# Repeated mask products on TensorE at the barriers, and the first square in another order

## The chip, the cores and the metric

The kernel runs on one core of a Trainium2 chip. The metric is the device time of one execution in microseconds (us), taken as the median of several runs. All products are exact enough for fp32 inputs, so most matrices are split into a high and a low part of type fp32r, and a product is three matrix products: high by high, low by high and high by low.

## The reference

`x` is (16, 512, 128): 16 batches, N = 512 nodes, D = 128. `adj` is (512, 512), sparse and symmetric in pattern. Four graph layers follow each other, each as `x = layernorm(x + layer(x))`. In short:

```
# layer 0: eight Euler steps of a diffusion
h = x @ fc_in_w.T + fc_in_b
for _ in range(8):
    f = 0.5 * sigmoid(alpha)[:, None] * (adj @ h - h) + h @ w_eff - h + x
    h = h + f / 8                      # w_eff = w * clip(d, 0, 1) @ w.T
# layer 1: two graph convolutions with ReLU, then LSTMs over windows of 1 to 4 nodes
# layer 2: normalized adjacency, 128 -> 256, batch norm, ReLU, 256 -> 128, batch norm
h = relu(batchnorm((A_hat @ x) @ W1.T + b1)); out = batchnorm(h @ W2.T + b2)
# layer 3: attention over 256 edges (src, dst), four heads
Y = segment_sum(softmax_by_src(leaky_relu(Xq[src] + Xq[dst]) . a + log(adj[src, dst])) * Xv[dst], src)
out = Y @ W_out.T
```

The changed kernel computes the same.

## The kernel before

`x` stays in SBUF from start to end. The program is four blocks, one after another, and all engines meet at a barrier between two blocks.

1. **`phase_operators`** (to about 63 us). It builds what layer 0 needs as operators. With L = kappa * adj + diagonal, it makes the transposed powers `LT0`, `LT1` (the square) and `LT2` (the third power), each split in high and low parts (`LT0h`, `LT0l`), and powers of the 128x128 operator R in `RP`. ACT makes the high parts, DVE the low parts of the powers (`split`), POOL the low part `Ll` of L itself. DVE also computes the row sums of adj (`row_sums`), from which the vectors `pair` and `U` are made. `l_power(r, j)` is one tile of a power: 4 chunks k, three products each, written out in the helper `product` (L65 to L67). The order of the tiles is a list (`order`), a bank of PSUM is a tile's place in it modulo 8, and PE's program below is written out by hand in that order: transpose of w (L465), transposes of L by chunk (L469), R (L474), `l_power(2, 0)`, and so on.
2. **`phase_main`** (about 63 to 832 us). Layers 0 and 1 and the first half of layer 2, in an order that a planner in the program sets. It also makes the edge masks `GZ` and `GsT` (names `z_GZ`, `z_GsT` in the profile), matrices of zeros and ones with few ones, of type fp32r. The change doesn't touch this block.
3. **`phase_batchnorm`** (about 832 to 871 us). DVE and POOL make the batch norm's scale and shift, ACT writes the normalized hidden layer `U` (L1875), PE multiplies it by `W2T` (L1861; both are f32, and such a product runs as two passes, each an instruction in the trace), DVE adds the bias (L1914) and takes statistics (L1907), and at the end makes scale and shift of the second batch norm (L1895 to L1901, with POOL). PE uses banks 4 to 7 here.
4. **`phase_attention`** (from 871 us). Layer 3, in an order from `first_part`, `slot` and `drain`; each engine walks the one list and takes its own items. For the part around the change: `z` is ACT's normalization of a batch (L2256), `T` PE's transposes of it (L2168), which DVE adds to X (L2328), then statistics (`s3`), variances (`v3`), POOL's root (`p3`, L2434), DVE's shift (`sh3`, L2350), the application on ACT and DVE (`ap3`, L2284 and L2380), the split of x (`xs`: ACT's high part, POOL's low part `aXL`), and `G`, PE's gather by the masks (L2177, eight products). T3 or G0 below is the item with its batch number.

Of the kernel before, what the change touches and what calls it, by code (L numbers as in the profile page):

```python
# [16 lines left out]
P = 128  # L17
# [45 lines left out]
def product(pe, out, lhs, rhs, start=True, stop=True):  # L63

    pe.matmul(out, lhs[0], rhs[0], start=start, stop=False)  # L65
    pe.matmul(out, lhs[0], rhs[1], start=False, stop=False)  # L66
    return pe.matmul(out, lhs[1], rhs[0], start=False, stop=stop)  # L67


def low_part(eng, out, full, high):  # L70
# [14 lines left out]
def phase_operators(nc, sh, d):  # L85
# [12 lines left out]
    C, D, N = sh.C, sh.D, sh.N  # L98
    with ExitStack() as ctx:
# [154 lines left out]
        def _(dve):  # L254
# [53 lines left out]
            for c in range(C):  # L308
# [6 lines left out]
            link(dve.tensor_scalar(dclip[:, :], dcol[:, :], 0.0, 1.0, ALU.max, ALU.min))  # L315
            dve.tensor_scalar(wTd[:, :], wT[:, :], dclip[:, 0:1], DT, ALU.mult, ALU.mult)\
                .then_inc(S["dve_tile"], 1)
            row_sums(0, 2)
            for j in range(C):
                split(f"LT{j}")  # L320
            copy("R", RP[:, 1, :], bank("R")[:, 0:D])
            link(row_sums(2, C))
            link(dve.tensor_tensor(pair[:, :, 1], sh.rs[:, :], kappa[:, :], ALU.mult))
            dve.wait_ge(S["memsets"], 5)
            link(dve.tensor_tensor(pair[:, :, 1], pair[:, :, 1], ldiag[:, :], ALU.add))
# [87 lines left out]
        def _(pe):  # L413
# [9 lines left out]
            def r_power(name, k, n, needs):  # L423
                begin(name, [needs])
                done(pe.matmul(bank(name)[:, 0:n * D], RP[:, k, :], RP[:, 1:n + 1, :], start=True, stop=True))

            def l_power(r, j):
                begin(f"L{r}T{j}", [] if r == 2 else [f"L{r - 1}T{C - 1}"])
                for k in range(C):
                    rows = slice(j * P, (j + 1) * P)  # L430
                    if r == 2 and j == 0:
                        pe.wait_ge(S["ll_done"], k + 1)
                        pe.wait_ge(S["dve_tile"], at[f"LT{k}"] + 1)
                    ins = product(pe, bank(f"L{r}T{j}"), (Lh[:, k, rows], Ll[:, k, rows]),
                                  (sh.LT[r - 2][0][:, k, :], sh.LT[r - 2][1][:, k, :]),
                                  start=(k == 0), stop=(k == C - 1))
                done(ins)
# [25 lines left out]
            pe.wait_ge(S["w_in"], 16)  # L463
            pe.wait_ge(S["idn"], 1)
            done(pe.transpose(bank("wT")[:, 0:D], w_nat[:, :], sh.ident[:, :]))  # L465
            for c in range(C):
                pe.wait_ge(S["l_done"], c + 1)
                for j in range(C):
                    ins = pe.transpose(bank(f"LT{j}")[:, c * P:(c + 1) * P], L[:, c, j * P:(j + 1) * P],  # L469
                                       sh.ident[:, :])  # L470
                    if c == C - 1:
                        done(ins)
# [1335 lines left out]
def phase_batchnorm(nc, sh, d):  # L1808
# [8 lines left out]
    with ExitStack() as ctx:  # L1817
# [35 lines left out]
        @block.tensor  # L1853
        def _(pe):
            def second(i, last):
                for b in range(QB):
                    n = QB * i + b
                    wait(pe, S["o_out"], n - QB + 1)
                    for j in range(J):
                        pe.wait_ge(S["u_done"], J * n + j + 1)  # L1860
                        ins = pe.matmul(sh.psum[:, 4 + b, :], sh.W2T[:, j, :], U[:, J * b + j, :], start=(j == 0),  # L1861
                                        stop=(j == J - 1))
                    ins.then_inc(S["o_mm"], 1)

            peeled(pe, NQ, second)

        @block.scalar
        def _(act):
# [86 lines left out]
def phase_attention(nc, sh, d, out):  # L1955
# [8 lines left out]
    with ExitStack() as ctx:  # L1964
# [34 lines left out]
        def first_part():  # L1999

            return [("z", 0), ("z", 1), ("T", 0), ("z", 2), ("s3", 0), ("v3", 0), ("p3", 0), ("T", 1), ("z", 3), ("s3", 1),
                    ("v3", 1), ("p3", 1), ("T", 2), ("z", 4), ("sh3", 0), ("ap3", 0), ("xs", 0), ("s3", 2), ("v3", 2),
                    ("sh3", 1), ("ap3", 1), ("xs", 1), ("p3", 2), ("T", 3), ("s3", 3)]

        def slot(k):
# [147 lines left out]
        @block.tensor  # L2153
        def _(pe):
            def begin_dve(item):
                n = dve_ring[item]
                wait(pe, S["dve_free"], n - len(DVE_BANKS) + 1)

            def begin_act(item):
                n = act_ring[item]  # L2160
                wait(pe, S["act_free"], n - len(ACT_BANKS) + 1)

            def turned(n):
                pe.wait_ge(S["z_done"], n + 1)
                begin_dve(("T", n))
                for c in range(C):
                    cols = slice(c * P, (c + 1) * P)
                    ins = pe.transpose(dve_bank(("T", n))[:, cols], tmp[:, n % QB, cols], sh.ident[:, :])  # L2168
                ins.then_inc(S["pe_dve"], 1)

            def gather(n):
                pe.wait_ge(S["xl_done"], n + 1)
                begin_act(("G", n))
                for c in range(C):
                    cols = slice(c * D, (c + 1) * D)
                    for part in (XH, XL):
                        ins = pe.matmul(act_bank(("G", n)), part[:, n % 2, cols], GZ[:, c, :, :],  # L2177
                                        start=(c == 0 and part is XH), stop=(c == C - 1 and part is XL))
                ins.then_inc(S["pe_act"], 1)

            def project_edges(n):
                pe.wait_ge(S["act_free"], act_ring["G", n] + 1)
                begin_act(("U", n))
                to = act_bank(("U", n))
                pe.matmul(to[:, 0:NE], WT[:, 0, :], Z[:, n % QB, 0:NE], start=True, stop=True)
                for k in range(K):
                    cols = slice(NE + k * P, NE + (k + 1) * P)
                    ins = pe.matmul(to[:, cols], Z[:, n % QB, cols], WT[:, 1, :], start=True, stop=True)
                ins.then_inc(S["pe_act"], 1)

            def scores(n):
                b = n % QB
                if b == 0:
                    wait(pe, S["sc_done"], n // QB)
                pe.wait_ge(S["lr_done"], n + 1)
                pe.matmul(sh.psum[0:R, 7, 0:NE], wide[:, R - NH - NH * b:2 * R - NH - NH * b], lr[:, b, :],
                          start=(b == 0), stop=(b == QB - 1)).then_inc(S["sc_mm"], 1)

            def attention_turned(g):
                to = dve_bank(("at", g))  # L2200
                pe.wait_ge(S["ex_done"], g + 1)
                begin_dve(("at", g))
                for k in range(K):
                    ins = pe.transpose(to[:, k * R:(k + 1) * R], s2[:, g, k * P:(k + 1) * P], sh.ident[0:R, 0:R])
                ins.then_inc(S["pe_dve"], 1)

            def denominators(g):
                to = dve_bank(("dn", g))
                pe.wait_ge(S["dve_free"], dve_ring["at", g] + 1)
                begin_dve(("dn", g))  # L2210
                for k in range(K):
                    for j in range(K):
                        ins = pe.matmul(to[:, k * R:(k + 1) * R], same[:, j, k * P:(k + 1) * P],
                                        exT[:, g, j * R:(j + 1) * R], start=(j == 0), stop=(j == K - 1))
                ins.then_inc(S["pe_dve"], 1)

            def scatter(n):
                pe.wait_ge(S["va_lo"], n + 1)
                begin_act(("S", n))
                for k in range(K):  # L2220
                    for part in (vah, val):
                        ins = pe.matmul(act_bank(("S", n)), part[:, n % QB, k, :], GsT[:, k, :],  # L2222
                                        start=(k == 0 and part is vah), stop=(k == K - 1 and part is val))
                ins.then_inc(S["pe_act"], 1)

            def project(n):
                pe.wait_ge(S["act_free"], act_ring["S", n] + 1)
                begin_dve(("P", n))
                for c in range(C):
                    cols = slice(c * P, (c + 1) * P)  # L2230
                    ins = pe.matmul(dve_bank(("P", n))[:, cols], Y[:, n % QB, cols], WT[:, 2, :], start=True, stop=True)  # L2231
                ins.then_inc(S["pe_dve"], 1)

            for kind, n in order:
                if kind == "T":
                    turned(n)
                elif kind == "G":
                    gather(n)
                elif kind == "U":
                    project_edges(n)  # L2240
                elif kind == "W":
                    scores(n)
                elif kind == "at":
                    attention_turned(n)
                elif kind == "dn":
                    denominators(n)
                elif kind == "S":
                    scatter(n)
                elif kind == "P":
                    project(n)  # L2250
# [278 lines left out]
```

## Time and profile before

| what | value |
|---|---|
| median of 3 runs | 1007.44 us (1007.18 to 1009.31) |
| the profiled execution | 1006.96 us |
| its span, first to last instruction | 1005.2 us |
| mean granted TensorE clock | 0.981 |
| PE busy | 922.8 us, 92% |
| PE weight loads | 792.2 us, 79% |
| DVE busy | 658.7 us, 66% |
| ACT busy | 546.1 us, 54% |
| POOL busy | 311.8 us, 31% |
| DMA | 31.62 MB, mean 31 GB/s |

The profile is one execution. A time in a row is counted from the start of the span. A row of the timeline is a group of like instructions: start, duration of the group, engine, line of the program, operation, output and input by name, shape, count, and in brackets how long the engine was idle before it and what it waited for. Durations of PE instructions include the way through the array, so the distance from one start to the next is what a product costs in a row of products. The granted clock is a share of full speed: 1.00 is 2.4 GHz, 0.50 is 1.2 GHz.

### The profile page before, as it was taken

How to read it: one execution, taken by the hardware profiler on the slowest of the kernel's cores; microseconds unless marked ns; L12 is line 12 of the kernel's file. 1: busy time of each engine (PE TensorE's matmuls, PEld its weight loads, DVE VectorE, ACT ScalarE, POOL GpSimd, SP SyncE). 2: the span in 40 equal slices, each digit the busy share in tenths (PEclk: the TensorE clock that was granted, in tenths of full speed). 3: DMA queues.
4: the chain of work that ended last, by engine and by line, in shares of the span. 5: the costliest groups of instructions: out<-in, count | busy, mean ns of one | idle time of the engine just before them, and what ended most of it. 6: DMA issues, size and time to landing. Idle time of an engine off the chain costs nothing. (4 is left out here: it accounts for less than half of the span.)

```text
span 1005.2 us, 14453 instructions
## 1 busy us (share of the span) xinstructions
PE 922.8 (92%) x5144; PEld 792.2 (79%) x5144; DVE 658.7 (66%) x1627; ACT 546.1 (54%) x1136; POOL 311.8 (31%) x290
## 2 busy tenths in 40 slices
PE   6999997999998999999999999899989987678994
PEld 4689986899997888998889899788778863356773
DVE  6664435445546646665655775698897876778877
ACT  2043224655645565554656464557667647466757
POOL 3011222331233233223323323224333220145663
PEclk9989999999999999999999999999999998889998
DMA  8030011001010100101010010301000000000014
GB/s 225 1 82 2 22 53 74 1 22 42 1 43 2 42 22 1 42 2 43 1 43 22 1 43 1 124 1 62 15 31 22 1 1 0 1 0 1 2 43 126
DMA packets 33994, 31.62 MB, mean 31 GB/s; under 512 B 8450, under 2 KB 28034, under 8 KB 33924
## 3 DMA queue, kind: packets, MB, share of 16 engines
q1 hardware_dynamic: 32900, 30.64, 9.9%
q8 instruction: 41, 0.67, 0.3%
q14 instruction: 29, 0.24, 0.1%
q10 hardware_dynamic: 960, 0.07, 0.1%
q0 software_dynamic: 64, 0.00, 0.0%
HBM read 22.83 MB, written 7.87 MB: 31 GB/s over the span
## 5 line engine op out<-in xcount | busy, mean ns | idle before, releaser
L1322 ACT ACTIVATE gates<-psum,gbias 128x256 f32<-128x256 f32 (+2 forms) x312 | 158.9, 565 | 63.5 <-PE psum L67 58.7
L65 PE MATMUL psum<-LS,WI 128*128 128x256 f32 (+2 forms) x312 | 104.1, 334 | 10.0 <-ACT gates L1322 6.3
L67 PE MATMUL psum<-LS,WI 128*128 128x256 f32 (+2 forms) x312 | 102.9, 330 | 0.0
L66 PE MATMUL psum<-LS,WI 128*128 128x256 f32 (+2 forms) x312 | 102.8, 330 | 0.0
L72 POOL TENSOR_TENSOR LS<-A,LS 128x512 fp32r<-128x512 f32 (+2 forms) x44 | 48.9, 1112 | 172.2 <-ACT LS L1307 172.1
L72 POOL TENSOR_TENSOR LS<-Hodd,LS 128x512 fp32r<-128x512 f32 (+2 forms) x44 | 48.8, 1109 | 147.5 <-ACT LS L1307 147.5
L72 DVE TENSOR_TENSOR yl<-psum,yh 128x512 fp32r<-128x512 f32 x58 | 39.6, 689 | 65.0 <-ACT yh L1264 44.2
L72 POOL TENSOR_TENSOR XSl<-X,XSh 128x512 fp32r<-128x512 f32 x32 | 42.3, 1324 | 115.8 <-ACT XSh L1259 115.8
L1329 ACT ACTIVATE tc<-cell 128x512 f32<-128x512 f32 (+2 forms) x88 | 45.3, 514 | 57.8 <-DVE cell L1617 33.7
L65 PEld LDWEIGHTS psum<-LS,WI 128*128 128x128 f32 x312 | 59.2, 190 | 19.5 <-POOL LS L72 10.2
L65 PE MATMUL psum<-B2h,LT2h 128*128 128x256 f32 x256 | 72.7, 284 | 1.0 <-DVE X L1435 1.0
L67 PE MATMUL psum<-B2h,LT2l 128*128 128x256 f32 x256 | 72.4, 283 | 0.0
L66 PE MATMUL psum<-B2l,LT2h 128*128 128x256 f32 x256 | 72.4, 283 | 0.0
L66 PEld LDWEIGHTS psum<-LS,WI 128*128 128x128 f32 x312 | 59.2, 190 | 5.0
L67 PEld LDWEIGHTS psum<-LS,WI 128*128 128x128 f32 x312 | 59.3, 190 | 4.2
L65 PE MATMUL psum<-LS,WH 128*128 128x256 f32 (+2 forms) x192 | 60.1, 313 | 0.0
L66 PE MATMUL psum<-LS,WH 128*128 128x256 f32 (+2 forms) x192 | 59.9, 312 | 0.0
L67 PE MATMUL psum<-LS,WH 128*128 128x256 f32 (+2 forms) x192 | 59.9, 312 | 0.0
L65 PE MATMUL psum<-Eh,yh 128*128 128x384 f32 x168 | 56.6, 337 | 0.0
L67 PE MATMUL psum<-Eh,yl 128*128 128x384 f32 x168 | 56.3, 335 | 0.0
L66 PE MATMUL psum<-El,yh 128*128 128x384 f32 x168 | 56.2, 335 | 0.0
L548 DVE BATCH_NORM_STATS2 nstats<-X 128x6 f32<-128x128 f32 x256 | 54.2, 278 | 0.4
(368 smaller groups left out, 2674.3 us busy)
## 6 DMA issues: line engine op xcount, KB each, us to landing
WI<-lstm_weights SPq DMA_DIRECT2D x14, 512.0 KB, 3.5
WH<-lstm_weights SPq DMA_DIRECT2D x11, 512.0 KB, 4.5
X<-in_x SPq DMA_DIRECT2D x16, 256.0 KB, 5.4
out<-X SPq DMA_DIRECT2D x16, 256.0 KB, 2.3
lstm_weights<-WI SPq DMA_DIRECT2D x4, 512.0 KB, 2.6
lstm_weights<-WH SPq DMA_DIRECT2D x3, 512.0 KB, 2.7
A<-in_adj SPq DMA_DIRECT2D x4, 256.0 KB, 4.5
z_A<-in_adj SPq DMA_DIRECT2D x1, 1024.0 KB, 5.2
```

What stands on the lines that cost most here:

```text
L65: pe.matmul(out, lhs[0], rhs[0], start=start, stop=False)
L66: pe.matmul(out, lhs[0], rhs[1], start=False, stop=False)
L67: return pe.matmul(out, lhs[1], rhs[0], start=False, stop=stop)
L72: return eng.tensor_tensor(out, full, high.bitcast(F32), ALU.subtract)
L548: return dve.bn_stats(self.stats[:, bass.ds(self.sh.C * n + c, 1), :], self.sh.X[:, c, bass.ds(n, 1), :])
L1322: act.activation(gates[:, gate, 0:n], sh.psum[:, gate, 0:n], ACT.Tanh if gate == G else ACT.Sigmoid, bias=gbias[:, p_ - 1, gate:gate + 1]) ...
L1329: act.activation(tcs[:, 0:n], cell[:, s % 2, 0:n], ACT.Tanh).then_inc(S["tanh_done"], 1)
```

## The change

A helper `keep_busy` issues n products into a bank that nothing reads at that time. It is called

- in `phase_operators`, five times after the transpose of w and twice before the transposes of chunk 2, identity by identity (f32, 128 columns), into the bank of `R2`, which a later product overwrites;
- in `phase_batchnorm`, 12 times before the first projection product and 16 times after the last, `GsT` by `GZ` (fp32r, 512 columns), into bank 0;
- in `phase_attention`, 24 times behind T2, as a new item `busy` of the list, into bank 7.

The first tile of the square (`first_square`) takes its four high-by-high products first and then the products with a low part. DVE's first two row sums move from before the low parts to behind them.

```
+def keep_busy(pe, out, lhs, rhs, n):
+    for _ in range(n):
+        pe.matmul(out, lhs, rhs, start=True, stop=True)
...
-            row_sums(0, 2)
             for j in range(C):
                 split(f"LT{j}")
             copy("R", RP[:, 1, :], bank("R")[:, 0:D])
-            link(row_sums(2, C))
+            link(row_sums(0, C))
...
+            def first_square(rows):
+                to, (high, low) = bank("L2T0"), sh.LT[0]
+                for k in range(C):
+                    pe.wait_ge(S["lh_done"], k + 1)
+                    pe.wait_ge(S["hi_done"], his.index(f"LT{k}") + 1)
+                    pe.matmul(to, Lh[:, k, rows], high[:, k, :], start=(k == 0), stop=False)
+                for k in range(C):
+                    pe.wait_ge(S["ll_done"], k + 1)
+                    pe.matmul(to, Ll[:, k, rows], high[:, k, :], start=False, stop=False)
+                    pe.wait_ge(S["dve_tile"], at[f"LT{k}"] + 1)
+                    ins = pe.matmul(to, Lh[:, k, rows], low[:, k, :], start=False, stop=(k == C - 1))
+                done(ins)
...
             def l_power(r, j):
                 begin(f"L{r}T{j}", [] if r == 2 else [f"L{r - 1}T{C - 1}"])
+                rows = slice(j * P, (j + 1) * P)
+                if r == 2 and j == 0:
+                    first_square(rows)
+                    return
                 for k in range(C):
-                    rows = slice(j * P, (j + 1) * P)
-                    if r == 2 and j == 0:
-                        pe.wait_ge(S["ll_done"], k + 1)
-                        pe.wait_ge(S["dve_tile"], at[f"LT{k}"] + 1)
...
             done(pe.transpose(bank("wT")[:, 0:D], w_nat[:, :], sh.ident[:, :]))
+            idle = bank("R2")[:, 0:P]
+            keep_busy(pe, idle, sh.ident[:, :], sh.ident[:, :], 5)
             for c in range(C):
+                if c == 2:
+                    keep_busy(pe, idle, sh.ident[:, :], sh.ident[:, :], 2)
                 pe.wait_ge(S["l_done"], c + 1)
...
+            masks = sh.GZ[:, 0, :, :]
+            keep_busy(pe, sh.psum[:, 0, :], sh.GsT[:, 0, 0:P], masks, 12)
             peeled(pe, NQ, second)
+            keep_busy(pe, sh.psum[:, 0, :], sh.GsT[:, 0, 0:P], masks, 16)
...
-                    ("v3", 1), ("p3", 1), ("T", 2), ("z", 4), ("sh3", 0), ...
+                    ("v3", 1), ("p3", 1), ("T", 2), ("busy", 0), ("z", 4), ("sh3", 0), ...
...
+                elif kind == "busy":
+                    keep_busy(pe, sh.psum[:, 7, :], GsT[:, 0, 0:P], GZ[:, 0, :, :], 24)
```

PE's own order at the start of `phase_operators`, before; `x16` are the transposes of L, and the three lines repeat for the four chunks:

```order
L465 MATMUL psum<-ident,w_nat 128x128
L469 MATMUL psum<-ident,L 128x128 x16
L474 MATMUL psum<-wT,wTd 128x128
L65 MATMUL psum<-LT0h,Lh 128x512
L66 MATMUL psum<-LT0l,Lh 128x512
L67 MATMUL psum<-LT0h,Ll 128x512
```

and now, with what each waits for (`hi_done` is ACT's high parts of the powers, `lh_done` and `ll_done` are the parts of L, `dve_tile` counts DVE's tiles):

```order
L73 MATMUL psum<-ident 128x128 x5
L491 MATMUL psum<-ident,L 128x128 [waits l_done]
L491 MATMUL psum<-ident,L 128x128 x3
...
L73 MATMUL psum<-ident 128x128 x2
L491 MATMUL psum<-ident,L 128x128 [waits l_done]
...
L496 MATMUL psum<-wT,wTd 128x128 [waits dve_tile]
L437 MATMUL psum<-LT0h,Lh 128x512 [waits hi_done,lh_done] x4
L440 MATMUL psum<-LT0h,Ll 128x512 [waits ll_done]
L442 MATMUL psum<-LT0l,Lh 128x512 [waits dve_tile]
```

Seven repeats are new, the four high products no longer wait for DVE, and the low ones alternate behind them.

PE's order at the end of the projection and the start of attention, now:

```order
L1883 MATMUL psum<-U,z_W2T 128x512 x8
L73 MATMUL psum<-z_GZ,z_GsT 128x512 x16
L1839 UNCONDITIONAL_BRANCH
L2178 UNCONDITIONAL_BRANCH
L2193 MATMUL psum<-ident,A 128x128 x12
L73 MATMUL psum<-z_GZ,z_GsT 128x512 x24
L2193 MATMUL psum<-ident,A 128x128 x4
L2202 MATMUL psum<-z_GZ,aXH 128x512
```

Before, the last eight projection products were followed by the two branches, 16 transposes in a row (T0 to T3) and G0. Now 16 repeats stand ahead of the branches and 24 between T2 and T3.

## Rows read from the trace of the kernel before

**Rows 1.** Busy time by stretch of TensorE: stretch, length, PE busy (count), granted clock, DMA.

```profile
13.45:18.98 5.53, 5.53 (x14) 1.00 1.20 290
...
834.77:841.59 6.82, 5.48 (x7) 0.50 0.00 0
...
868.90:875.73 6.83, 3.67 (x16) 0.50 0.00 1
875.73:879.14 3.41, 0.00 (x0) 1.00 0.00 0
879.14:885.97 6.83, 4.51 (x13) 0.50 0.00 0
```

**Rows 2.** Timeline of PE in the first 20 us.

```profile
7.90 1.97 PE L469 MATMUL psum<-ident,L 128*128 128x128 f32 x8 [1.04 <-DVE L L312]
10.36 1.12 PE L469 MATMUL psum<-ident,L 128*128 128x128 f32 x4 [0.49 <-DVE L L312]
11.57 0.79 PE L474 MATMUL psum<-wT,wTd 128*128 128x128 f32 x2
13.45 0.77 PE L65 MATMUL psum<-LT0h,Lh 128*128 128x512 f32 x1 [1.08 <-DVE LT0l L72]
14.01 0.63 PE L66 MATMUL psum<-LT0l,Lh 128*128 128x512 f32 x1
...
18.28 0.63 PE L67 MATMUL psum<-LT0h,Ll 128*128 128x512 f32 x1
...
19.54 0.40 PE L67 MATMUL psum<-LT0h,Ll 128*128 128x512 f32 x1
19.77 0.39 PE L65 MATMUL psum<-LT0h,Lh 128*128 128x512 f32 x1
```

**Rows 3.** Timeline of the other engines, 10.5 to 14.5 us.

```profile
10.40 1.11 DVE L316 TENSOR_SCALAR wTd<-wT,dclip 128x128 f32<-128x128 f32 x1
10.88 2.06 ACT L244 ACTIVATE LT0h<-psum 128x512 fp32r<-128x512 f32 x4
11.44 1.27 DVE L298 TENSOR_REDUCE rs<-A 128x1 f32<-128x512 f32 x2
...
12.63 2.47 DVE L72 TENSOR_TENSOR LT0l<-psum,LT0h 128x512 fp32r<-128x512 f32 x4
```

**Rows 4.** Waits of PE between 13 and 62 us; the answer's other row is the 1.08 above.

```profile
PE psum L446 <- DVE U L72: 0.9, 1, 0.9
```

**Rows 5.** Timeline from the barrier at 832 us into the projection.

```profile
832.54 1.04 DVE L1895 BATCH_NORM_AGGREGATE bmv<-z_st 128x2 f32<-128x96 f32 x2 [0.32 <-PEq L621]
...
835.24 7.15 ACT L1875 ACTIVATE U<-z_hidden,bsh,bsc 128x512 f32<-128x512 f32 x10 [3.75 <-DVE bsh L1901]
...
836.11 14.13 PE L1861 MATMUL psum<-U,z_W2T 128*128 128x512 f32 x26 [5.34 <-ACT U L1875]
...
854.80 11.75 PE L1861 MATMUL psum<-U,z_W2T 128*128 128x512 f32 x27
```

**Rows 6.** Timeline from the projection's end over the barrier at 871 us.

```profile
861.67 4.88 PE L1861 MATMUL psum<-U,z_W2T 128*128 128x512 f32 x11
...
870.48 0.16 DVE L1901 TENSOR_TENSOR bsh<-z_par,bsh 128x1 f32<-128x1 f32 x1
...
872.02 3.67 PE L2168 MATMUL psum<-ident,A 128*128 128x128 f32 x16 [5.47 <-ACT A L2256]
```

**Rows 7.** Timeline of the start of attention.

```profile
881.46 0.80 PE L2177 MATMUL psum<-z_GZ,aXH 128*128 128x512 f32 x1 [5.77 <-POOL aXL L72]
...
882.25 0.68 DVE L2328 TENSOR_TENSOR X<-psum,X 128x512 f32<-128x512 f32 x1
...
884.66 1.00 POOL L2434 TENSOR_TENSOR n3scale<-n3work,const 128x4 f32<-128x4 f32 x1
...
885.04 1.50 PE L2168 MATMUL psum<-ident,A 128*128 128x128 f32 x8
...
886.13 1.29 DVE L2328 TENSOR_TENSOR X<-psum,X 128x512 f32<-128x512 f32 x2 [2.29 <-PE psum L2168]
...
887.34 0.15 DVE L2350 SCALAR_TENSOR_TENSOR n3shift<-n3work,n3scale 128x4 f32<-128x4 f32 x1
```

More of the change, by code:

```diff
@@ L2001, in first_part @@
             return [("z", 0), ("z", 1), ("T", 0), ("z", 2), ("s3", 0), ("v3", 0), ("p3", 0), ("T", 1), ("z", 3), ("s3", 1),
-                    ("v3", 1), ("p3", 1), ("T", 2), ("z", 4), ("sh3", 0), ("ap3", 0), ("xs", 0), ("s3", 2), ("v3", 2),
+                    ("v3", 1), ("p3", 1), ("T", 2), ("busy", 0), ("z", 4), ("sh3", 0), ("ap3", 0), ("xs", 0), ("s3", 2), ("v3", 2),
                     ("sh3", 1), ("ap3", 1), ("xs", 1), ("p3", 2), ("T", 3), ("s3", 3)]
```

## The prediction

> **What bounds the kernel now.** I read the granted clock by stretch first [rows 1], then the timeline of TensorE (PE) at the places where the clock is low. After its start the kernel is a chain in which PE is busy 92% of the span, so time that PE loses in front of its own work is mostly time of the span. The clock column says 0.50 from 834.77 to 841.59, from 868.90 to 875.73 and from 879.14 to 885.97 [rows 1]. Each of these begins after a pause of PE and ends after a run of steady work: 836.11 to 841.59 (5.5 us), 872.02 to 875.73 (3.7), 881.46 to 885.97 (4.5) [rows 5, 6, 7].
>
> At the very start the column misleads. It says 1.00 for 13.45 to 18.98, but ten products from 14.01 to 18.28 are 0.427 us apart, and the same shape is 0.23 us apart at 19.54 to 19.77 [rows 1, 2]. 512 columns in 0.427 us are the 1.2 GHz level, in 0.23 us the 2.4 GHz level; so this stretch is at half clock too, and the clock rose near 18.98, after 5.5 us of steady work. The Trainium skill, "TensorE: Matmul & The Clock Gate", Part 1, says that half clock is the default state, released by activity, and warns that recorded clock events can be unreliable; the spacing agrees. By the column instead, the first term below would be only the wait removed, 1.4 us.
>
> **Term 1, the start.** Before, PE ends the transposes of L at 11.48, computes R from 11.57 in two passes, and then waits 1.08 us for the first low part, since DVE does two row sums (1.27 us) ahead of it [rows 2, 3]. The first square starts at 13.45. Now its four high products come first, and need only ACT's high parts: the first is there at 11.48 (10.88 plus 0.6), the fourth at 12.94. R holds PE to 12.0, so the square starts at 12.0, 1.45 us earlier. The low parts start on DVE when wTd is done at 11.51, and the fourth is there near 14.0 (2.47 us for four [rows 3]); at 0.427 us per product PE asks for it near 16.7, at full clock near 14.5. All four row sums (2.5 us) now stand between R's copy and U. DVE is at R's copy at 14.0, so U is there near 17.7; PE wants it behind the second square, near 18 or later. That is close but covered; if PE runs at full clock from 12.2 it may wait some tenths.
>
> The repeats themselves: five 128-column f32 products after the transpose of w take about 0.43 us each (R, the same form, has its two passes 0.2 us apart [rows 2]), 2.1 us from about 2.9 to 5.1, before L is there at 5.7: no cost. Two more take 0.85 us between 8.75 and 9.6. They push the last transposes from 10.36 to about 10.45, and R waits for wTd at 11.51 anyway: at most 0.1 us.
>
> If the clock still rises at 18.98, 1.45 us of added half-clock work is worth 0.7 us. Each us by which it rises earlier adds 0.5 us. With the repeats PE is steadily busy from 7.90 to 11.3, and after a pause of 0.2 us from 11.57 on. The runs before a rise were 3.7 to 5.5 us, 4.8 in the mean: counted from 11.57 the rise is at 16.4 (gain 2.0), counted from 7.90 at 12.7 (gain 3.6, where the low parts begin to bind). I take a rise near 15.2: 0.7 + 0.5 x 3.8 = **2.6 us**. Bounds 0.7 and 3.6. Behind this, PE has one more wait up to 62 us, 0.89 us for U [rows 4], which hangs on PE's own products, and so moves with them. Nothing later waits for a time of day: the shift passes the barrier near 63.
>
> **Term 2, the second projection.** PE ends at 830.77 (836.11 less 5.34), engines leave the barrier at about 832.5, ACT gives its first U after 835.24, one per 0.72 us [rows 5]. Twelve mask products (form 128x512 fp32r, 0.23 us at full clock [rows 2]) fill 832.6 to 835.4. Two pauses of 1.8 and 0.7 us stay where one of 5.3 was. At full clock a pass takes 0.43 us (11.75 us for 27 [rows 5]), two per product, 0.87 against ACT's 0.72 per U, so PE is the limit from its first product on, and the cold 5.48 us [rows 1, 5] hold 2.74 us of full-clock work. **2.7 us** gained; bounds 2.7, and 0.9 if the clock falls in the 1.8 us pause: repeats then take 0.427 us each, end at 837.7 (1.6 late plus some 0.2), with the clock rising about then.
>
> **Term 3, the start of attention.** Sixteen mask products behind the last projection take 3.7 us, from 866.2 to 869.9; DVE's statistics end at 870.64 [rows 6]. So PE reaches the barrier 0.6 us before DVE: no cost. At half clock they would take 6.8 us and hold the barrier up by 2.4. A pause of 2.1 us stays to 872.02 in place of 5.47 [rows 6]. Transposes at full clock are ready about 0.4 us earlier (four at 0.21 us, halved), and DVE starts at 872.8 in place of 873.2. Then 24 mask products, 5.6 us at full clock from 873.9, end at 879.5. T3 stands behind them; DVE wants it at 882.25 [rows 7], so 2.7 us of slack cover them. G0 waits for POOL's low part at 881.46 less 0.4, and its eight products take 1.9 us in place of 3.6 [rows 7]. T4 and T5 stand behind G0, and DVE waits 2.29 us for T4 [rows 7]: this wait nearly goes. Late next is POOL's root, 885.66 less 0.4; the shift that DVE made at 887.34 comes at about 885.3 to 885.5. **1.9 us**. If the clock falls in the 2.1 us pause, the repeats themselves warm it: they end near 881.5, G0 starts 0.5 late but is quick, gain 1.2. Bounds 0 and 2.0.
>
> **Sum.** 2.6 + 2.7 + 1.9 = 7.2 us. The profiled execution took 1006.96 us, so 999.8; the median of the three runs lies 0.5 above it, and against that I say **1000.2 us**. The removed waits are no engine's work elsewhere, but low-clock stretches that the change doesn't touch can fall elsewhere when everything shifts; one us either way.
>
> **Rivals.**
> *Pauses too long.* The clock falls in both remaining pauses. For: it fell 2.4 us after PE's last product at 866.55 (861.67 plus 4.88) [rows 1, 6]. Against: at 830.77 it took 4.0 us. Terms 0.9 and 1.2, with 2.6 at the start: 1002.7.
>
> *Start only shifts.* The clock at the start rises no sooner, since neither the identity products nor the steadier run bring the rise forward; 0.7 to 1.4 us in place of 2.6: 1001.7.
>
> *Quiet repeats (slower).* Products of mask by mask, nearly all zeros, do not hold the clock up, and it is low through them. Then the twelve take 5.1 us and end 1.6 us late; at the end of the projection about 0.3 us hangs over DVE; and the 24, from 874.8, take 10.2 us to 885.1. T3 and G0 then start near 885.5, 4.5 us late where before T3 was in time. 1.6 + 0.3 + 4.5 less 1.4 at the start is +5.0: 1012.4. It decides if the 24 are spaced 0.427 us to their end: above about 0.35 us apart they outlast the slack of T3. Against: G0 has the same masks as moving operand and the clock rose within it [rows 1, 7]; but there the other operand was dense.
>
> *No net change.* Time shifted forward is lost again in a longer cold stretch behind the barrier near 63 or in the pause of attention, or U comes late. The Trainium skill, same page and part, reports that one kernel had 6, 11 or 14 cold products from run to run, and puts the whole ramp below 1% of a span; here 12 of the first square were cold, within that. By 6 alone the cold loss at the start would be 1.2 us. Time 1006.5. No row shows such a second execution.
>
> **Chances.** Forecast 0.60 (its own range 998.0 to 1002.0), pauses too long 0.16, start only shifts 0.10, no net change 0.08, slower 0.06. A measurement of this kernel tells 0.2%, 2.0 us, from no change: faster 0.86, same 0.08, slower 0.06. The range 997.2 to 1004.3 takes in the forecast with its bounds and the two rivals of partial gain, and leaves out the last two.
>
> **What would show it.** In the changed profile: the square's first product near 12.0 and 0.23 us spacing from about 15; granted clock 1.00 from 830 to 870, first projection product 0.75 us behind the twelve, U products 0.43 us per pass at once; 24 repeats 0.23 us apart, ended before 880; G0 in 1.9 us; DVE's wait for T4 under 0.5 us. Wrong would be: repeats spaced 0.427 us throughout (slower), PE behind DVE at a barrier, DVE or PE waiting for U near 18.

## The result, and the profile after

Eight executions of each kernel: median 1000.98 us (998.36 to 1004.92) with the change, 1007.31 us without it. The medians are 6.3 us apart. The ratio of all executions is 0.9926, 95% interval 0.9899 to 0.9954: faster by 4.6 to 10.2 us, under 1%. The forecast was 1000.2 us. The profiled execution took 1001.52 us. Of the later executions of the kernel before, two lie far outside the rest (1170.59 and 3196.63 us) and are in no comparison.

The head of its page, against 922.8 us of PE and a span of 1005.2 us before:

```profile
span 999.7 us, 14585 instructions
PE 934.2 (93%) x5210; PEld 803.4 (80%) x5210; DVE 658.8 (66%) x1627; ACT 545.4 (55%) x1136; POOL 312.3 (31%) x290
```

PE is busy 11.4 us longer in a span that is 5.5 us shorter: the repeats are added work. The stretches of the granted clock in the changed kernel (columns as in [rows 1]):

```profile
12.38:15.57 3.19, 3.19 (x7) 0.50 1.19 299
15.67:18.98 3.31, 3.31 (x17) 1.00 1.20 290
60.19:63.45 3.26, 3.26 (x16) 0.50 0.23 58
476.44:479.85 3.41, 3.41 (x11) 0.50 0.00 0
732.53:735.94 3.41, 3.18 (x11) 0.51 0.00 0
810.91:814.32 3.41, 3.41 (x9) 0.51 0.00 0
829.50:868.90 39.40, 35.24 (x97) 1.00 0.01 1
868.98:872.38 3.40, 3.40 (x12) 0.50 0.00 0
...
971.38:974.78 3.40, 3.40 (x18) 0.50 0.27 77
```

The whole projection with both pauses around it, 829.50 to 868.90, now runs at the 2.4 GHz level. At the start of attention the clock still falls, at 868.98, but comes back 3.4 us later, where before it was low from 868.90 to 875.73 and again from 879.14 to 885.97 [rows 1]. Three cold stretches (stretches at 0.50) are new against the profile before: near 476, near 811 and near 971.

The timeline of PE at the start, the counterpart of [rows 2]:

```profile
2.95 2.34 PE L73 MATMUL psum<-ident 128*128 128x128 f32 x10
6.01 1.97 PE L491 MATMUL psum<-ident,L 128*128 128x128 f32 x8 [0.72 <-DVE L L318]
7.77 1.06 PE L73 MATMUL psum<-ident 128*128 128x128 f32 x4
8.62 0.70 PE L491 MATMUL psum<-ident,L 128*128 128x128 f32 x4
11.14 0.66 PE L491 MATMUL psum<-ident,L 128*128 128x128 f32 x4 [1.82 <-DVE L L318]
...
12.38 2.22 PE L437 MATMUL psum<-LT0h,Lh 128*128 128x512 f32 x4 [0.36 <-ACT LT0h L250]
...
16.84 0.38 PE L430 MATMUL psum<-RP 128*128 128x128 f32 x2
```

The seven repeats are fourteen passes, in 2.34 and 1.06 us with the way through the array; 2.1 and 0.85 were costed. In this execution they did bring the clock up: four transposes take 0.70 us at 8.62, against 1.12 us for four at 10.36 [rows 2], and the two passes of R take 0.39 us, against 0.79. But PE waits 1.82 us for the last chunk of L, the clock falls at 12.23, and the first seven products of the square are cold again. The steady run the forecast counted on, from 7.90 on, did not come about.

PE from the second barrier on:

```profile
831.46 3.00 PE L73 MATMUL psum<-z_GZ,z_GsT 128*128 128x512 f32 x12 [1.77 <-PEq L643]
835.03 27.73 PE L1883 MATMUL psum<-U,z_W2T 128*128 128x512 f32 x64 [0.57 <-ACT U L1900]
862.20 4.23 PE L73 MATMUL psum<-z_GZ,z_GsT 128*128 128x512 f32 x16
868.23 2.67 PE L2193 MATMUL psum<-ident,A 128*128 128x128 f32 x12 [1.80 <-ACT A L2283]
870.55 6.60 PE L73 MATMUL psum<-z_GZ,z_GsT 128*128 128x512 f32 x24
876.99 0.60 PE L2193 MATMUL psum<-ident,A 128*128 128x128 f32 x4
877.35 0.48 PE L2202 MATMUL psum<-z_GZ,aXH 128*128 128x512 f32 x1
```

The pause of 5.34 us [rows 5] is now 1.77 and 0.57 us. The 64 passes of the projection take 27.73 us, 0.43 us apart from the first. The sixteen repeats end at 866.43, and DVE's last instruction of the block ends at 866.85, the first row below, so they hold up nothing. The 24 repeats, the first few of them slow, end at 877.15, just before G0's input is there: POOL's low part ends at 877.21. DVE at these places:

```profile
866.69 0.16 DVE L1926 TENSOR_TENSOR bsh<-z_par,bsh 128x1 f32<-128x1 f32 x1
...
879.91 1.37 DVE L2355 TENSOR_TENSOR X<-psum,X 128x512 f32<-128x512 f32 x2 [0.27 <-PE psum L2193]
881.51 0.16 DVE L2377 SCALAR_TENSOR_TENSOR n3shift<-n3work,n3scale 128x4 f32<-128x4 f32 x1 [0.22 <-POOL n3scale L2461]
```

DVE's wait for T4 fell from 2.29 us [rows 7] to 0.27, and the shift for batch 2 now waits for POOL's root, as forecast.

### The profile page after: what moved, and what is told of

It reads as the page before. It is cut to its first block and busy times, and to the rows that moved or that the text cites. A ratio compares the mean times of both kernels' runs of the same rounds, so it can differ in the third digit from the quotient of the medians.

```text
span 999.7 us, 14585 instructions
## 1 busy us (share of the span) xinstructions
PE 934.2 (93%) x5210; PEld 803.4 (80%) x5210; DVE 658.8 (66%) x1627; ACT 545.4 (55%) x1136; POOL 312.3 (31%) x290
```

## Six stages, read from every profile

One profile can't separate terms of 2 us from the scatter of single executions, which is as large. The kernel before alone had times near 1005.4, 1007.4, 1010.4 and 1012.6 us in 34 executions beside the first experiments. So each profile is cut at the same instructions. Each column is the difference of two start times in it:

- start: 0 to the R product behind the square's first tile
- second: from there to PE's first product of the main block
- main: to the last widening product of that block
- projection: its first product to T0
- head: T0 to DVE's shift for batch 2
- tail: from there to the end of the span

Between the main block's last product and the projection's first lie 5.74 us that no column holds (7.37 in `e7_rows4`).

```
kernel            start  second   main   projection   head    tail
before            18.71   44.52  767.14     35.91     15.32  117.86
e12_before_again  18.74   44.45  774.87     35.83     15.27  117.90
e1_start          15.94   43.37  771.62     34.84     14.80  117.89
e5_square         16.48   43.35  767.17     35.90     15.32  117.84
e6_ident          18.47   44.63  768.97     34.73     14.74  117.82
e2_projection     17.70   43.36  769.10     33.21     15.38  117.91
e3_attention      17.88   43.37  769.11     34.84     13.27  120.49
after             16.84   43.35  769.09     33.20     13.28  118.19
e4_full           16.46   43.35  769.35     33.21     13.30  119.60
e11_full_again    16.05   43.37  768.88     33.20     13.25  119.50
e9_plus           15.36   43.55  769.87     33.20     13.24  117.83
e10_plus          15.35   44.03  771.45     33.20     13.25  118.57
e7_rows4          15.83   43.38  771.54     36.69     18.89  119.60
e8_double         16.20   43.36  769.22     33.21     18.30  120.77
```

The main block, which the change doesn't touch, took 767.1 to 774.9 us. What differs there is how often the clock fell: once in `before` (736) and `e5_square` (732), three times in `after` (476, 732, 811), five times in `e1_start` and `e7_rows4`. From one fall to three is 2.0 us, to five 4.4 us, so a fall there costs 1.0 to 1.1 us.

## The experiments

### The parts alone

`e1_start` keeps the identity repeats, the square's new order and the moved row sums, and has no mask products:

```
-            keep_busy(pe, sh.psum[:, 0, :], sh.GsT[:, 0, 0:P], masks, 12)
-            keep_busy(pe, sh.psum[:, 0, :], sh.GsT[:, 0, 0:P], masks, 16)
-                    ("v3", 1), ("p3", 1), ("T", 2), ("busy", 0), ("z", 4), ...
+                    ("v3", 1), ("p3", 1), ("T", 2), ("z", 4), ...
```

> The start part alone: seven identity repeats, the first square with its high products first, DVE's row sums behind. Theory (terms add): 1.5 to 3 us faster than before; in the profile the second tile of the square starts near 17.0 instead of 18.98, and this lead is kept to the first barrier. Rival (the start is absorbed later): the lead is seen at 20 us and gone at 63 us, and the time is within 0.5 us of before. The cold stretches at 836 and 879 stay as before.

Measured: ratio 0.9979 (0.9962 to 0.9996), 2.1 us faster. Start stage 15.94 us against 18.71, and the lead stays: second stage 43.37. The rival of an absorbed start falls. The cold stretches at the barriers did not stay as before, though nothing there was changed: the one in the projection was 3.4 us long and not 6.8, and that stage took 34.84 us.

`e2_projection` has only the first of these three edits left in, and the start as before.

> Only the twelve mask products ahead of the projection. Theory: granted clock stays 1.00 from 832 to 868, the 64 projection passes take 27.7 us instead of 30.4, 2.7 us faster than before. Rival (another cold stretch takes its place): passes as quick, but the time less than 1 us faster.

Measured: ratio 0.9986 (0.9965 to 1.0007). Its two rows of PE:

```profile
832.33 3.01 PE L73 MATMUL psum<-z_GZ,z_GsT 128*128 128x512 f32 x12 [1.77 <-PEq L647]
...
835.90 27.73 PE L1887 MATMUL psum<-U,z_W2T 128*128 128x512 f32 x64 [0.57 <-ACT U L1903]
```

The mechanism is exactly as stated: 27.73 us of passes. The stage is 33.21 us; in the six profiles without the twelve repeats it is 34.7 to 35.9, 35.3 in the mean. So the term is 2.1 us in the mean, and 2.7 where the cold stretch is as long as in the first profile. The time, 1.4 us faster, agrees with that, but its interval reaches no change, so the time alone does not decide against the rival.

`e3_attention` has only the sixteen and the 24 repeats.

> Only the sixteen mask products behind the projection and the 24 behind T2. Theory: G0 starts at once at full clock, DVE's shift for batch 2 comes 16 us behind the barrier's exit less 2, DVE waits under 0.5 us for T4; 1.5 to 2 us faster than before. Rival (the repeats hold T3 and G0 up): G0 starts later than before relative to the barrier and nothing is gained.

Measured: ratio 1.0000 (0.9979 to 1.0022): nothing. Yet the head stage is 13.27 us against 14.7 to 15.4 in the six kernels without these repeats, the forecast 1.9 us. What went wrong stands in the tail, 120.49 us against 117.9. Three cold stretches of it:

```profile
894.04:897.44 3.40, 3.40 (x9) 0.50 0.00 0
917.92:924.76 6.84, 6.84 (x24) 0.50 0.00 0
975.96:979.36 3.40, 3.40 (x18) 0.50 0.27 77
```

The clock falls there in the thin part of attention, where PE waits for DVE and POOL again and again for 0.5 to 1.3 us. Not every fall costs time. The falls of all profiles, in us behind the shift for batch 2, with the start of the last of the sixteen gathers and the end of the span counted from the same shift (a fall 110 to 113 us behind it, near the end of the span, is in every profile and left out):

```
profiles                               falls (length)                last gather    tail
before, e12_before_again, e5_square    none                          72.0 to 72.1   117.84 to 117.90
e1_start, e6_ident                     90 (3.4)                      72.0 to 72.1   117.82, 117.89
after                                  90 (3.4)                      72.0           118.19
e2_projection, e9_plus                 9 (3.4)                       72.1           117.91, 117.83
e10_plus                               10 (3.4)                      72.8           118.57
e4_full, e11_full_again, e7_rows4      35 (3.4), 90 (6.8)            72.7           119.50 to 119.60
e3_attention, e8_double                10 (3.4), 34 (6.8), 92 (3.4)  74.2 to 74.3   120.49, 120.77
```

The fall near 894, the first of the three rows, costs nothing: two profiles have one there and the old tail. The fall 34 to 35 us behind the shift delays the later gathers by 0.7 us where it is 3.4 us long, and by 2.2 where it is 6.8; with a 6.8 us stretch near 90 another 1.0 to 1.1 is lost.

In the six profiles without these repeats the tail was 117.82 to 117.91 us; in the five with the 24 full-height repeats as the change has them (`e3_attention`, `after`, `e4_full`, `e11_full_again`, `e9_plus`) it was 117.83 to 120.49, 119.1 in the mean. So 1.2 of the 1.9 us are given back on average, more than all of it in `e3_attention` and nothing in `e9_plus`. Without the repeats DVE's shift for batch 2 came 1.0 to 2.0 us behind a rise of the clock in all six, since G0, whose end releases it, was itself slow until that rise. With them it stands in no fixed relation to a rise. That this is why the costly falls never came before is an argument from these profiles, not shown by an edit.

`e4_full` is the changed kernel.

> The changed kernel again, as the sum to hold the three parts against on one chip. Theory (terms add): 6 to 8 us faster than before, the sum of the three parts within 2 us. In its profile the clock falls in other pauses of the main block than in the run before the prediction, by up to two more or fewer stretches of 1.6 to 1.7 us each.

Measured: ratio 0.9944 (0.9925 to 0.9963), 5.6 us faster; the three parts alone gave 2.1, 1.4 and 0.0. The whole is just under the 6 to 8 us expected. The sum, 3.5 us, is 2.1 below the whole, just outside the margin of 2 given and inside what their intervals leave. There were cold stretches near 476, 732 and 811 as in `after`.

### What does the work at the start

`e5_square` is `e1_start` without the seven identity repeats.

```
-            keep_busy(pe, idle, sh.ident[:, :], sh.ident[:, :], 5)
-                if c == 2:
-                    keep_busy(pe, idle, sh.ident[:, :], sh.ident[:, :], 2)
```

> The start part without its identity repeats: only the order of the square and the moved row sums. Theory (the repeats bring the clock up earlier): the square starts near 12.2, 1.2 us earlier than before, but the clock rises only after four to six us of it, and the second product of R (the one behind the square's first tile) starts at 16.8 to 17.6, later than the 15.9 to 16.8 with repeats. Rival (the order alone does it): as early as with repeats, 16.4 or sooner.

`e6_ident` is the reverse, also without mask products: the identity repeats, with the square and the row sums of before.

```
+            row_sums(0, 2)
             for j in range(C):
                 split(f"LT{j}")
...
-            link(row_sums(0, C))
+            link(row_sums(2, C))
...
-                    first_square(rows)
+                    for k in range(C):
+                        pe.wait_ge(S["ll_done"], k + 1)
+                        pe.wait_ge(S["dve_tile"], at[f"LT{k}"] + 1)
+                        ins = product(...)
```

> The identity repeats with the square and the row sums in the old order. Theory: the square starts at 13.2 to 13.5 as before, and the second product of R starts near 17.0 to 17.8, against 17.7 to 18.7 in the kernels with the old start. Rival (the repeats do nothing): 17.7 or later and a cold square of at least ten products.

PE in `e5_square`, then in `e6_ident`:

```profile
11.51 0.80 PE L493 MATMUL psum<-wT,wTd 128*128 128x128 f32 x2
11.96 2.05 PE L437 MATMUL psum<-LT0h,Lh 128*128 128x512 f32 x4
```

```profile
9.38 1.44 PE L498 MATMUL psum<-ident,L 128*128 128x128 f32 x8 [0.94 <-DVE L L318]
11.48 0.80 PE L503 MATMUL psum<-wT,wTd 128*128 128x128 f32 x2 [0.66 <-DVE wTd L322]
13.36 0.77 PE L65 MATMUL psum<-LT0h,Lh 128*128 128x512 f32 x1 [1.08 <-DVE LT0l L78]
```

Without repeats the square starts at 11.96, where the forecast put it (12.0), and the start stage is 16.48 us, sooner than the 16.8 to 17.6 expected and close to the 16.4 of the rival, that the order alone does it. With the repeats alone it is 18.47, with eleven cold products in the first square: that is what the rival named, that the repeats do nothing. In that execution the clock was up early, eight transposes in 1.44 us against 1.97 in [rows 2], and was low again by R, whose two passes take 0.80 us. The four kernels with the old start have 18.71, 17.70, 17.88 and 18.74, mean 18.3; the eight with the whole new start 15.35 to 16.84, mean 16.0. By the one profile of `e5_square`, the order of the square and the moved row sums carry about 1.8 of 2.3 us. What the identity repeats add, at most 0.5 us, is within the scatter of single profiles and stays open.

### Rows, not time: the price of repeats that do not count

`e7_rows4` narrows all mask repeats to 4 partition rows, and changes nothing else.

```
-            masks = sh.GZ[:, 0, :, :]
+            masks = sh.GZ[0:4, 0, :, :]
...
-            keep_busy(pe, sh.psum[:, 0, :], sh.GsT[:, 0, 0:P], masks, 12)
+            keep_busy(pe, sh.psum[:, 0, :], sh.GsT[0:4, 0, 0:P], masks, 12)
...
-                    keep_busy(pe, sh.psum[:, 7, :], GsT[:, 0, 0:P], GZ[:, 0, :, :], 24)
+                    keep_busy(pe, sh.psum[:, 7, :], GsT[0:4, 0, 0:P], GZ[0:4, 0, :, :], 24)
```

> All three groups of mask repeats with 4 partition rows instead of 128, the same count and columns. Theory of the change as first stated (TensorE only has to be busy): as the changed kernel, clock 1.00 through the projection, 33.2 us from the first projection product to T0. Rival (products of few rows do not hold the clock, as in the stretch of 4-row products from 57.3 us on, at whose end it fell while PE was busy): the clock falls during the twelve, these take up to 5.1 us and the projection starts up to 1.6 us late and is cold for some us; the 24 take up to 10.2 us and G0 comes 12 to 14 us behind T0 instead of 9.1; total about 1006 to 1011 us. This is also the price of the rival of quiet repeats in the prediction.

PE in its timeline, the 4-row products written as 4*128, and the granted clock of two stretches:

```profile
832.92 5.27 PE L73 MATMUL psum<-z_GZ,z_GsT 4*128 4x512 f32 x12 [1.77 <-PEq L643]
838.12 7.15 PE L1883 MATMUL psum<-U,z_W2T 128*128 128x512 f32 x10
...
868.38 5.29 PE L73 MATMUL psum<-z_GZ,z_GsT 4*128 4x512 f32 x16
...
877.56 10.60 PE L73 MATMUL psum<-z_GZ,z_GsT 4*128 4x512 f32 x24
888.10 1.12 PE L2193 MATMUL psum<-ident,A 128*128 128x128 f32 x4
```

```profile
832.00:842.30 10.30, 9.38 (x17) 0.55 0.01 2
870.70:891.20 20.50, 19.36 (x54) 0.50 0.00 1
```

One execution, 1015.14 us, above the 1006 to 1011 expected; its main block, which the edit doesn't touch, was one of the long ones, and one execution of the kernel before beside it took 1014.22 us, so only the stages tell here. The clock was low for 20.5 us in a row although PE was busy 19.4 of them. It fell at 870.67 within the sixteen, with PE busy: most of the first ten start 0.23 us apart, the last six 0.427. The twelve took 5.27 us and the 24 took 10.60, T0 to the shift became 18.9 us, and the projection 36.7 us plus 1.6 us before it. These are the forecast's prices of its slower rival: 5.1 us, 10.2 us, and T3 and G0 some 4.5 us late. Only the question whether the change's own repeats count was answered the other way. The Trainium skill, "TensorE: Matmul & The Clock Gate", section "LDWEIGHTS (loading the stationary operand)", says that the row count does not matter for the time of a weight load. The trace agrees: at the low clock a load of 4 rows took 0.326 us, and a full-height one of the same mask 0.331 (the first slow ones of the 24 in `after`). The products, too, are 0.427 us apart at that clock at either height. But for the clock the height mattered in this pair of runs.

`e8_double` doubles the 24.

```
-                    keep_busy(pe, sh.psum[:, 7, :], GsT[:, 0, 0:P], GZ[:, 0, :, :], 24)
+                    keep_busy(pe, sh.psum[:, 7, :], GsT[:, 0, 0:P], GZ[:, 0, :, :], 48)
```

> 48 instead of 24 repeats behind T2; the rest as changed. Theory (the 24 are covered since DVE wants T3 only later): the 48 end 5.6 us later, T3 is 4 to 5 us late for DVE, G0 starts 14.2 to 14.8 us behind T0 instead of 9.1 and DVE's shift for batch 2 about 17.5 to 18.5 instead of 13.3: 4 to 5 us slower than the changed kernel. Rival (PE time is free there): no more than 1 us later.

PE, then DVE:

```profile
870.04 12.01 PE L73 MATMUL psum<-z_GZ,z_GsT 128*128 128x512 f32 x48
881.89 0.60 PE L2193 MATMUL psum<-ident,A 128*128 128x128 f32 x4
```

```profile
882.53 0.69 DVE L2355 TENSOR_TENSOR X<-psum,X 128x512 f32<-128x512 f32 x1 [4.90 <-PE psum L2193]
```

G0 came 14.5 us behind T0 and the shift 18.3 us, 5.0 us later than with 24. So 24 repeats are free and 48 are not. How much slack is left behind the 24 depends on the clock: in `after`, where the first ones are slow, next to none, and in `e3_attention`, with the clock up, PE still waited 1.05 us for POOL ahead of G0.

### A version with more of it

`e9_plus` adds repeats in two pauses of the main block:

```
+                if b == 11 and j == 0:
+                    begin(n)
+                    keep_busy(pe, bank(n), sh.WT[0][:, 0, :], bn["AhTh"][:, 0, :], 11)
...
+                if q == NQ - 1 and k == first_step(3) + 1:
+                    wait(pe, gate_act[G], NS * q + uses(k, G))
+                    keep_busy(pe, sh.psum[:, G, :], sh.WT[0][:, 0, :], bn["AhTh"][:, 0, :], 10)
                 pe.wait_ge(S["xs_done"], NS * q + k + 1)
```

> The changed kernel with repeats in two more pauses, both in the main block: ten ahead of the second LSTM step of window 3 in the last quarter (the pause of 2.6 us near 733), eleven ahead of the widening of batch 11 (the pause of 2.7 us near 810). Full-height operands, into a bank that the next product overwrites. Theory (a pause of TensorE over about 2 us costs a cold stretch of 3.4 us, 1.6 to 1.7 us of time, in most executions): the clock no longer falls near 732 and 810, the main block takes 1.6 to 3.3 us less, and the time is 1.5 to 3.3 us below the changed kernel's. Rival (the fall is only moved on): another cold stretch within 20 us, less than 1 us gained.

Two rows of PE, and one stretch of the clock:

```profile
732.99 4.13 PE L73 MATMUL psum<-z_AhTh,z_WTh 128*128 128x512 f32 x10 [2.49 <-ACT gates L1350]
736.96 0.32 PE L65 MATMUL psum<-LS,WI 128*128 128x340 f32 x1
```

```profile
806.00:815.00 9.00, 8.81 (x38) 1.00 0.00 0
```

Ratio to before 0.9936 (0.9915 to 0.9956), median 1000.2 us, beside `e11_full_again` with 1000.4 and 0.9944: no difference that can be told. The main block took 769.87 us against 768.88 in `e11_full_again`, where 1.6 to 3.3 us less were expected: in this execution the clock also fell near 153 and 638. And by the main blocks above a fall there costs 1.0 to 1.1 us, not 1.6 to 1.7. The pause of about 2 us in the theory is no measured limit either: a pause of 1.80 us ahead of T0 was followed by a fall in `after`, and one of 2.74 us near 812 by none in the first profile of before. Near 810 it did what was expected. Near 733 it failed: the free bank came only after 2.49 us, when ACT had read the gates. So the ten stood behind the pause and not in it, cold, 4.1 us long, with the LSTM step behind them. The trace of the changed kernel had named POOL as the last releaser of that pause; ACT's release was nearly as late, and did not show:

```profile
732.76 0.63 PE L65 MATMUL psum<-LS,WI 128*128 128x340 f32 x1 [2.58 <-POOL LS L78]
```

`e10_plus` adds three mask products ahead of G2 to G5.

```
             def gather(n):
-                pe.wait_ge(S["xl_done"], n + 1)
                 begin_act(("G", n))
+                if 2 <= n <= 5:
+                    keep_busy(pe, act_bank(("G", n)), GsT[:, 0, 0:P], GZ[:, 0, :, :], 3)
+                pe.wait_ge(S["xl_done"], n + 1)
```

> As e9_plus, and three mask products ahead of each of G2 to G5 in attention, where TensorE waits 0.7 to 1.2 us for POOL's low part. Theory: they fit in the waits, the clock falls less often between 880 and 920 and the part behind the shift for batch 2 stays at 117.8 to 118.5 us, where the other runs had up to 120.8: 0 to 2 us below e9_plus. Rival (TensorE has no room there): the gathers come later, 0.5 to 2 us slower than e9_plus.

Ratio 0.9929 (0.9905 to 0.9954), median 1000.38: the same as `e9_plus`. Its tail was 118.57 us, just outside the 117.8 to 118.5 expected, with one cold stretch near 893. `e9_plus` has one at the same place and 117.83; in `e10_plus` the gathers behind the added products come up to 1.8 us later than there, and 0.7 of that stays to the last gather. In this profile the cost is that of the rival, that TensorE has no room there; the times don't decide it.

`e11_full_again` is the changed kernel once more.

> The changed kernel once more, beside e9_plus and e10_plus on their chip. Expected 5 to 8 us below the kernel before by all theories; its profile has cold stretches near 732 and 810 again if these pauses lose the clock as a rule and not by chance.

Measured: 0.9944 (0.9921 to 0.9967), and cold stretches at 475, 731 and 810 again. Over all fourteen profiles the clock fell at 731 to 740 in every one, near 811 (818 in `e12_before_again`) in ten of the twelve that have no repeats there, and near 476 in seven.

`e12_before_again` is the kernel before.

> The kernel before, for a second profile. Theory (the profile before was a lucky one in the main block): a main block of about 769 us from its first transpose to the last widening product, with cold stretches near 735 and 812, where the first profile had 767.1 and one of them. Rival (the change adds them): 767.1 again.

One execution, 1014.61 us, above what was expected: a main block of 774.87 us with falls near 163, 313, 644, 740 and 818, the one near 740 lasting some 10 us. It has the start, projection and head of the first profile to 0.1 us. So neither the long main block nor its falls belong to the change, and the first profile of before was a short one in the main block, as is `e5_square` with 767.17.

## Why the prediction was right, point by point

- **What bounds it.** Right. PE's pauses ahead of its own work set the time at both barriers, and the lead from the start was carried through: `e1_start`, `e5_square` and the full kernels have second stages of 43.35 to 43.55 us (44.03 in `e10_plus`), no longer than the 44.52 of before.
- **Term 1, 2.6 us.** Measured 2.3 (stage means 18.3 and 16.0). The sum was right for a reason that was half wrong. The square started 1.3 us earlier, against 1.45 worked out (11.80 to 12.38 in the eight profiles with the whole new start, 13.36 to 13.53 in the five with the old one). The step that failed is the steady run from 7.90 on: it had PE busy from the repeats into R. In `after` the last chunk of L came at 11.14, not at 10.36, behind a pause of 1.82 us, and the clock that the repeats had raised was down again for the square; in six other profiles PE paused 0.71 to 0.84 us ahead of the third chunk. Only in `e10_plus` did the clock stay up into the square; in the others it rose at 13.0 to 15.6 us, where 15.2 was taken. [rows 2] show the chunk timings of one execution, which the forecast took as fixed. It took the rise at 18.98 as fixed too, and the kernels with the old square and without the identity repeats had it at 16.5 to 19.7.
- **Term 2, 2.7 us.** Measured 2.1 in the mean; 2.7 was the value of one profile, whose cold stretch was among the longest. The pause of 1.8 us that stays did not cost the clock in any of seven profiles with the twelve full-height repeats.
- **Term 3, 1.9 us.** In the head stage 1.9, exactly as costed, with POOL's root next in line. But the term as a whole is 0.6 in the mean, as the tail got 1.2 us longer. The prediction followed the chain only to the shift for batch 2 and took it that what follows is unchanged. It had named "low-clock stretches elsewhere" as one us either way; in the tail they went one way only.
- **Second stage.** About 0.6 us gained that no term held (44.1 in the mean of five profiles with the old square, 43.5 in nine with the new one). It is not the square as such: `e2_projection` and `e3_attention` have the old one and 43.36 and 43.37. The four long second stages, 44.03 to 44.63, are those in which the clock fell 2.5 to 3.9 us ahead of the stage's end, near 57 to 61; in the ten others it fell at most 1.6 us ahead. What decides that place no edit shows.
- **Sum.** 2.3 + 2.1 + 0.6 + 0.6 = 5.6 us by stage, against 7.2 forecast and 5.6, 5.6 and 7.4 us measured in three comparisons. All three intervals hold 5.6. That the median of 1000.98 us came within 0.8 of the forecast is in part luck: the stages sum to 1.6 us less than forecast, the terms fell short in the projection and the tail, and a gain that no term held made up for some of it.
- **Rivals.** "Pauses too long" was half true: the clock fell close behind T0's start in `after`, `e4_full` and `e8_double`, and the repeats raised it again, as worked out; in `e3_attention`, `e9_plus`, `e10_plus` and `e11_full_again` it did not fall there. "Quiet repeats" fell: masks held the clock as well as any product. Its price was confirmed by `e7_rows4`. "No net change" described a real thing, falls at other places, but of the wrong size for the whole. "Start only shifts" gave the identity repeats and the steadier run no effect; for the repeats the runs leave that open, and the start stage still gained 2.3 us and not 0.7 to 1.4.

## What to carry to other kernels

Filling a pause with idle products pays where PE waits for something that is not PE, where the next work is long and limited by PE, and where the free bank is there at the start of the pause; count what the engine behind can wait, and end the repeats before that. Follow the gain past the place it is made: here 1.2 of the 1.9 us won in the head were lost again in the tail, in the mean of five profiles, and one profile alone could have shown none of it. When single executions scatter by more than the terms, cut several profiles into stages at fixed instructions, and judge a term by its own stage; whole times then only confirm the sum.

## What the runs showed of the hardware

- Products of 4 partition rows did not keep TensorE at the 2.4 GHz level: 0.50 granted over 20.5 us with PE busy 19.4 (`e7_rows4`), where with full-height products of the same masks the clock was 1.00 from 829.5 to 868.9 (`after`), and all but the first five of the 48 in `e8_double` ran 0.23 us apart. The masks are nearly all zeros, and full height held the clock nonetheless. The 4-row side rests on one execution.
- The Trainium skill, "TensorE: Matmul & The Clock Gate", Part 1, says that the count of cold products at a start varies from run to run, with 6, 11 and 14 as examples. It does here: of the twelve products of the first square, seven, eight and five started before the rise in three profiles of the changed kernel (`after`, `e4_full`, `e11_full_again`).
- Whether the clock falls behind a pause of the main block can differ between executions, and no run shows what decides it: the wait of 2.74 us near 812 kept the clock in the first profile and lost it in the changed kernel's. Two executions of the kernel before took 767.14 and 774.87 us in that block.
